# Feed-forward weights quantised in units beside the attention batches, kept in DRAM and loaded in the last one

## What is computed

```python
def fp4_quant_dequant(x):
    xb = x.reshape(shape[:-1] + (shape[-1] // BLOCK, BLOCK))
    scale = jnp.max(jnp.abs(xb), axis=-1, keepdims=True) / 6.0
    scale = jnp.maximum(scale, jnp.float32(1e-12))
    xn = xb / scale
    idx = jnp.searchsorted(_MID, jnp.abs(xn))
    q = _GRID[idx] * jnp.sign(xn) * scale
...
gate = fp4_linear(x, w_gate)
y = fp4_linear(x, w_up)
h = jax.nn.silu(gate) * y
return fp4_linear(h, w_down)
```

## Time and profile before

| | |
|---|---|
| Median of 3 runs | 4076.98 us (4074.86 to 4081.36) |
| The profiled execution | 4073.83 us |
| Its span | 4072.0 us |
| Mean granted TensorE clock | 0.966 |
| PE busy | 3790.2 us (93%) |
| DVE busy | 2592.0 us (64%) |
| ACT busy | 1211.1 us (30%) |
| POOL busy | 930.6 us (23%) |
| Moved by DMA | 302.38 MB, mean 74 GB/s |

### The profile page before, as it was taken

The page is one execution under the profiler, slowest core; times in us unless marked ns, Lnnn a source line. Parts: engine busy times, 40 slices in busy tenths (PEclk is TensorE's granted clock), DMA queues, the critical chain, the costliest instruction groups (busy, mean ns, idle before and its releaser), DMA issues. The chain is left out here.

```text
span 4072.0 us, 63435 instructions
## 1 busy us (share of the span) xinstructions
PE 3790.2 (93%) x21836; PEld 2715.4 (67%) x21836; DVE 2592.0 (64%) x3683; ACT 1211.1 (30%) x2295; POOL 930.6 (23%) x464
## 2 busy tenths in 40 slices
PE   7999999999999999999999727999999999999998
PEld 5556556556565565565565316888888888888887
DVE  4664654655645646646556496777777777777776
ACT  2441432532523514414325222222222222222221
POOL 0451550642533614605516300000000000000000
PEclk9999999999999999999999858999999999999999
DMA  4424424325335244244243220000111010011110
GB/s 150 114 65 148 99 75 146 76 93 141 73 107 132 58 139 116 67 151 94 74 146 76 71 70 16 31 31 31 34 33 33 31 31 31 31 31 31 36 32 28
DMA packets 161754, 302.38 MB, mean 74 GB/s; under 512 B 41072, under 2 KB 43120, under 8 KB 161520
## 3 DMA queue, kind: packets, MB, share of 16 engines
q1 hardware_dynamic: 143088, 265.79, 23.4%
q10 hardware_dynamic: 18432, 33.56, 2.5%
HBM read 196.61 MB, written 101.13 MB: 73 GB/s over the span
## 5 line engine op out<-in xcount | busy, mean ns | idle before, releaser
L1275 PE MATMUL f_ps<-wgu,xqt 128*128 128x512 f32 (+1 forms) x4608 | 994.5, 373 | 17.4 <-DVE h L1130 14.5
L1275 PEld LDWEIGHTS f_ps<-wgu,xqt 128*128 128x128 f32 x4608 | 842.6, 188 | 154.3 <-DVE h L1130 29.9
L668 ACT ACTIVATE pt<-ps_st 128x512 f32<-128x512 f32 (+3 forms) x1152 | 551.7, 527 | 659.8 <-PE ps_st L777 511.9
L502 DVE TENSOR_REDUCE mx<-ps_s 128x1 f32<-128x640 f32 (+3 forms) x576 | 553.4, 961 | 237.9 <-PE ps_s L757 234.7
L439 POOL TENSOR_TENSOR stage<-stage,pt 128x1536 f32<-128x1536 f32 (+2 forms) x176 | 518.2, 2944 | 15.5 <-POOL stage L439 0.5
L1285 PE MATMUL f_ps_o<-wd,hqt 128*128 128x512 f32 x2112 | 512.1, 395 | 2.2 <-DVE hqt L1137 2.2
L437 POOL TENSOR_TENSOR stage<-pt 128x1792 f32<-128x1792 f32 x64 | 258.5, 4040 | 1034.5 <-ACT pt L668 1034.5
L1285 PEld LDWEIGHTS f_ps_o<-wd,hqt 128*128 128x128 f32 x2112 | 392.3, 189 | 80.8 <-DVE hqt L1137 2.6
L728 PE MATMUL ps_dense<-arena,wa 128*128 128x512 f32 x1536 | 401.5, 407 | 8.9 <-DVE rob L550 7.5
L502 DVE TENSOR_REDUCE mx<-ps_dense 128x1 f32<-128x512 f32 x448 | 219.0, 489 | 216.9 <-PE ps_dense L757 211.8
L728 PEld LDWEIGHTS ps_dense<-arena,wa 128*128 128x128 f32 x1536 | 284.7, 192 | 74.1 <-issue 11.7
(11 more groups left out here) (121 smaller groups left out, 4786.9 us busy)
## 6 DMA issues: line engine op xcount, KB each, us to landing
qk_scratch<-stage SPq DMA_DIRECT2D x128, 512.0 KB, 3.0
stack<-qk_scratch SPq DMA_DIRECT2D x192, 256.0 KB
arena<-qk_scratch SPq DMA_DIRECT2D x192, 256.0 KB
xs<-in_L_attn_x SPq DMA_DIRECT2D x64, 256.0 KB, 3.2
rob<-in_L_attn_x ACTq DMA_DIRECT2D x64, 256.0 KB, 2.8
acc_scratch<-rob ACTq DMA_DIRECT2D x64, 256.0 KB, 2.2
xt<-in_L_attn_x SPq DMA_DIRECT2D x64, 256.0 KB, 2.6
at<-acc_scratch SPq DMA_DIRECT2D x64, 256.0 KB, 2.6
```

Of the source, the lines that this page charges most:

```text
L502: nc.vector.tensor_reduce(mx[:, h * ST + q:h * ST + q + 1], scores_bank(p, n)[:, 0:(q + 1) * P], axis=AX.X, op=ALU.max, negate=True).then_ ...
L668: nc.scalar.activation(exps(kt)[:, h, q - kt * P:q - kt * P + n], ps_st[:, w % ST_RING, 0:n], ACT.Exp, scale=SCALE).then_inc(st_exp, 1)
L1275: last = nc.tensor.matmul(ps[:, [0, 1, 1][c], gu, 0:n], xqt[:, a, k], wgu[:, b, gu, k, f:f + n], start=i == 0, stop=i == len(terms) - 1)
```

## The change

The weight stage between the parts is gone, and both parts are one block: `attention` and `feed_forward` now return a function for each engine, and `layer` calls them one after the other inside one block. SBUF tensors are placed by hand (`Memory`), so that tensors of the second part lie over those of the first that are done.

- *Raw copy.* At the start ACT issues six DRAM to DRAM copies of w_gate, w_up and w_down into `raw_scratch`, which holds 33 units of 128 x 512 (8.65 MB in all). SP waits for all six (`q_raw`) at the head of each batch.
- *Units.* Each batch quantises four units, the last one five, with working space in `pt`, which is free outside the head pairs. Two (three in the last batch) stand beside the Q/K/V products: scaled and rounded by DVE in two pieces (`scale_unit`, `round_unit`), ACT's magnitude between them, four PE transposes into `ps_y` (`transpose_unit`), halves by ACT and DVE (`high_of_unit`, `low_of_unit`). Two stand beside the projection. SP stores those beside the products, ACT those beside the projection, each as two halves of 256 KB in `wq_scratch`. SP loads a unit from `raw_scratch`.
- *Loads in the last batch.* ACT issues the loads of `wgu` (11.5 MB) in three pieces: before the head pairs, before pair 6 and before pair 7, and nine of eleven units of `wd` after the last denominators, ahead of the third `res` load. SP loads the last two units of `wd` behind the projection. The first tile of x is quantised beside pair 7.
- *Layout.* `wgu` is now unit by unit; a gate/up product reads four (or three) pieces of 128 columns, 2 KB apart.

The core of the diff, white space apart:

```diff
@@ sync @@
+            sp.wait_ge(q_raw, 6 * DMA)
+            sp.wait_ge(q_lo, ONE + b * PER_BATCH)
+            for i in range(2):
+                load_unit(i)
...
             for i, (g, r, c) in enumerate(QK):
...
+                if i == 6:
+                    store_unit(0)
+                    if final:
+                        load_unit(2)
+                if i == 7:
+                    store_unit(1)
+                if i == 9 and final:
+                    store_unit(2)
...
+            sp.wait_ge(den_full, ONE + b * PAIRS + PAIRS)
+            for i in beside_projection(final):
+                load_unit(i)
@@ vector @@
+            def scale_unit(i):
...
+                link(n, 1, nc.vector.tensor_reduce(sc[:, 0], in_blocks(w), axis=AX.X, op=ALU.max, apply_absolute_value=True))
+                link(n, 2, nc.vector.tensor_scalar(sc[:, 1], sc[:, 0], 1.0 / 6.0, MIN_SCALE, ALU.mult, ALU.max))
+                link(n, 3, nc.vector.reciprocal(sc[:, 2], sc[:, 1]))
+                link(n, 4, nc.vector.tensor_scalar(sc[:, 2], sc[:, 2], TIE, None, ALU.mult))
+                nc.vector.tensor_tensor(in_blocks(t), in_blocks(w), wide(sc[:, 2]), ALU.mult).then_inc(q_t, 1)
...
+                if use == ("V", 2):
+                    scale_unit(0)
+                if use == ("QK", 4):
+                    round_unit(0)
+                if use == ("QK", 5):
+                    scale_unit(1)
+                if use == ("V", 3):
+                    round_unit(1)
+                if use == ("QK", 6):
+                    low_of_unit(0)
+                if use == ("QK", 7):
+                    low_of_unit(1)
+                if final:
+                    if use == ("V", 4):
+                        scale_unit(2)
+                    if use == ("V", 5):
+                        round_unit(2)
+                    if use == ("QK", 9):
+                        low_of_unit(2)
...
             for k in range(ST):
                 add(k)
+                if k == 0:
+                    scale_unit(one)
+                if k == 1:
+                    round_unit(one)
+                if k == 2:
+                    scale_unit(two)
+                if k == 3:
+                    round_unit(two)
+                if k == 4:
+                    low_of_unit(one)
+                if k == 6:
+                    low_of_unit(two)
@@ scalar @@
+        act.dma_start(raw[0:FC].rearrange("u p n -> (u p) n"), w_gate).then_inc(q_raw, DMA)
+        act.dma_start(raw[FC:2 * FC].rearrange("u p n -> (u p) n"), w_up).then_inc(q_raw, DMA)
+        for r in range(KC):
+            act.dma_start(raw[2 * FC:UNITS, :, r * P:(r + 1) * P],
+                          w_down[r * P:(r + 1) * P].rearrange("p (u n) -> u p n", n=P)).then_inc(q_raw, DMA)
...
+            if final:
+                act.wait_ge(v_done, ONE + b * ST + ST)
+                act.wait_ge(qk_lo, ONE + b * NQK + NQK)
+                shared.load_gate_up(act, 0)
             for p in range(PAIRS):
+                if final and p == PAIRS - 2:
+                    shared.load_gate_up(act, 1)
+                if final and p == PAIRS - 1:
+                    shared.load_gate_up(act, 2)
@@ tensor @@
+                if use == ("V", 3):
+                    transpose_unit(0)
+                if use == ("V", 4):
+                    transpose_unit(1)
+                if use == ("QK", 8) and final:
+                    transpose_unit(2)
...
+                if k == 3:
+                    transpose_unit(one)
+                if k == 5:
+                    transpose_unit(two)
@@ feed_forward @@
+    PIECES = [[(0, 0, 2 * FC), (1, 0, 2)], [(1, 2, 16)], [(1, 18, 4)]]
-                        last = nc.tensor.matmul(ps[:, [0, 1, 1][c], gu, 0:n], xqt[:, a, k], wgu[:, b, gu, k, f:f + n],
+                    last = nc.tensor.matmul(ps[:, [0, 1, 1][c], gu, 0:n].rearrange("p (j n) -> p j n", n=P), xqt[:, a, k],
+                                            wgu[:, b, gu * FC + f // P:gu * FC + (f + n) // P, k * P:(k + 1) * P],
```

More of the change, by code:

```diff
@@ new lines, in attention, with w_stage, stack, bank @@
+    DMA = 16
+    LOADS = 7
+    LOADS_AFTER = {6: 5, 7: 2, **{i: 1 for i in range(9, NQK)}}
+    def w_stage(k):
+        return pt[:, (k % 2) * 3 * D:(k % 2 + 1) * 3 * D]
+    def stack(p):
+        s = p % SLOTS
+        return stack01[:, s] if s < 2 else arena[:, s - 2]
+    def bank(kind, i):
+        return ps_dense[:, DN[kind, i] % 2]
+    ob, res = rob[:, 0:2], rob[:, 2:4]
+    dn = ob[:, 0]
+    tail = rob[:, 1:4].rearrange("p a n -> p (a n)")
+    def v_head(t, p, h):
+        first = (2 * p + h) * HD
+        return v[:, t, first:first + HD]
@@ new lines, in body @@
+                    if u == Y_UNIT and p and p < PAIRS - 1:
+                        divide(p - 1)
+            divide(PAIRS - 2)
+            invert_last()
+            divide(PAIRS - 1)
+            if not final:
+                for t in range(XR):
+                    low_of_x(b + 1, t)
+            else:
+                shared.low_of_first(dve)
+            one, two = beside_projection(final)
+            for k in range(ST):
+                add(k)
+                if k == 0:
[10 more added lines that the diff above has]
+                    low_of_unit(two)
@@ L829, in body @@
[L829 to L849 removed]
+                            if kt < summed(p):
+                                src, cols = by_tile(sums(h))[:, s::2], slice(0, QC)
+                            else:
+                                src, cols = exps_of_parity(kt, h, s), y_cols(kt, s)
@@ new lines, in body @@
+                    transposed_scores(p, u, parts - 1)
+                    for n in tiles[ahead:]:
+                        scores(*n)
+                    mask_transposed(p, u, parts - 1)
+                    for n in tiles[ahead:]:
+                        mask_scores(*n)
+            for kt in range(RINGED, ST):
+                times_v(PAIRS - 1, kt)
+            denominators(PAIRS - 1)
+            if not final:
+                for t in range(XR - 1):
+                    transpose_x(b + 1, t)
+            else:
+                shared.transpose_first(pe)
@@ new lines, in feed_forward, with load_gate_up @@
+    x_d, h_d = sem("f_x_d"), sem("f_h_d")
+    PIECES = [[(0, 0, 2 * FC), (1, 0, 2)], [(1, 2, 16)], [(1, 18, 4)]]
+    GATE_UP_LOADS = sum(len(piece) for piece in PIECES)
+    DOWN_LOADS = 6
+    assert 2 * FC == 22 and FC == 11
+    def load_gate_up(act, n):
+        for half, first, units in PIECES[n]:
+            act.dma_start(wgu[:, half, first:first + units].bitcast(F32),
+                          wq[half, :, first:first + units]).then_inc(shared.wgu_in, DMA)
+    shared.load_gate_up = load_gate_up
```

2053 lines of the change are left out of this document (1050 added, 1003 removed).

## The result

The changed kernel takes 4010.22 us (median of 4 runs, 4001.83 to 4014.22) beside 4076.57 for the kernel before on the same chip (4074.86 to 4081.36): a ratio of 0.9833, 95% interval 0.9815 to 0.9850, 66 us or 1.7% less. The forecast was 4023, its range 3978 to 4062. The profiled execution took 4001.83 us (span 4000.0), the shortest of the four.

What follows compares the result with a forecast made beforehand. Before: PE bounds attention and feed-forward, DVE the 156.6 us weight stage between. Terms -159.0 + 49 + 37 + 19 = -54 took the span from 4072.0 to 4018, forecast 4023 us, range 3978 to 4062.

Steps and rivals of the forecast that it cites:

- The gap: Weight quantisation between last projection product and first gate/up product, DVE-bound: all of it goes, -156.6 us.
- The cold clock: First 48 gate/up products: PE no longer starts cold, 11.04 us instead of 13.43, -2.4 us.
- Units beside the batches: Quantising units beside Q/K/V and projection: 3.6 + 1.3 + 1.2 = 6.1 us a batch, +49 over eight; bounds 19 and 72.
- 0.52 MB at 233 GB/s is 2.25 us: Two 256 KB stores ahead of QK7's store delay the first stack's loads 2.25 us, part of a 3.6 us later wait.
- The rooms on DVE: DVE has time for units: 22 us of PE against 16 of DVE in Q/K/V, 2.74 idle of each 3.43 in projection.
- DVE becomes the bound: Rival: units' 5.75 us of DVE and ACT lie on PE's path; all exposed, +87 us, 4164; chance 0.05.
- The copy: Start of batch 0: SP's wait for the 8.65 MB raw copy stops PE from 48.83 to 84.2, +37 us; bounds 18 and 50.
- What would show it: Signs: PE idle about 49 to 84 until QK2's low half; stack wait 5 to 6 us; batches 6 us longer.
- loads block ACT: Rival: in the last batch a large load's issue holds ACT or SP, +20 to 40 us, 4040 to 4062; chance 0.12.
- The last batch: Extra there: third unit 7.5 and 0.6, down loads 5, gate/up loads 6, together +19 us; bounds 4 and 40.
- side costs are small: Rival: copy near 415 GB/s and stack wait hardly later, 3965 to 4000 us; chance 0.22.
- gate/up's operand layout: Rival: wgu's strided pieces slow gate/up by 13 ns a product, 60 us over 4608 products; chance 0.04.

Runs made afterwards that it cites:

- s4_stores_later: Changed kernel with the stores of units 0 and 1 in batches 0 to 6 issued behind QK10's store: 3992.45 us, 0.9780 of the kernel before.
- s1_flat_down: Changed kernel with w_down's four rearranging copies made one flat copy of the same 2.9 MB: 4006.41 us, 0.9815 of the kernel before.
- s1 to s4: Four single edits of the changed kernel: s1_flat_down, s2_no_copy, s4_stores_later, and s3, with SP's copy wait and first unit loads behind QK3's store (4001.53 us).
- l1_third_unit_early: Changed kernel with the final batch's third unit loaded behind QK5's store instead of QK6's: 4001.72 us, 0.9815 of the kernel before.
- s2_no_copy: Changed kernel without raw weight copies or waits for them, units loaded from rows of x instead: 3979.66 us, 0.9748 of the kernel before.
- c1_copy_in_parts: Changed kernel copying only gate and up at the start, one down unit per batch, final down units loaded directly: 3994.82 us, 0.9801 of the kernel before.
- c3_direct_units: Changed kernel with three units per batch straight from the weights, a seven-unit copy, and stores, loads and first-x quantisation re-placed: 3943.20 us, 0.9665 of the kernel before.

## Why the prediction was right, and where it was not

**The gap, -156.6 us:** it is gone whole. **The cold clock, -2.4:** from the first gate/up product to the one that started at 2516.49 before, the same work takes 47.00 us instead of 48.69, so 1.7 came; over the whole feed-forward 0.2 is left.

**Units beside the batches, 6.1 us each, 49 in all:** too high; batches 1 to 6 grew by 3.9. The first score, forecast 3.6 us later in its batch, came 2.7 later. The step that failed is the term "0.52 MB at 233 GB/s is 2.25 us": with the stores moved away (s4_stores_later) the first score comes 1.2 us sooner. That the first stack load goes out 1.3 later was right (1.4 us, though in part by the new wait for QK0's half). The 1.3 us for the clock behind it were 0.5: first score to projection takes 209.2 us instead of 208.7. The 1.2 beside the projection were 0.7. A set of four transposes shows as 0.60 us, but in the projection the product behind it starts 0.44 us after it. The rooms on DVE (22 us against 16; 2.74 of each 3.43) held: no wait of PE that a unit's own pieces on DVE explain shows in batches 0 to 6, and the rival "DVE becomes the bound" fell.

**The copy, +37, plus a batch's 6.1:** batch 0 grew by 29.8, of which 3.9 are a batch's, so 26. The mechanism was in part another one. PE did not stand from 49 to 84 and go on with QK2's half, as "What would show it" has it: it stood from 42.3 to 65.9 until QK0's half was there, then 3.75 us for QK2's, 27.4 in all where 35.4 was forecast. V0 started at 78.00 where 84.2 was forecast. Two errors. The copy was over sooner: SP's wait ends at 70.2, 35 us after the first issue, 247 GB/s for 8.65 MB with the landing in it, where 76.5 was forecast. (By the 207 to 214 GB/s of the Trainium skill, DMA: Bandwidth & Descriptors, Latency and other measured facts, it would have been 41 us; the whole copy went faster.) The forecast took 218 GB/s for all of it. The queues moved 407 from 36 to 44 and 319 from 44 to 54, with the flat copies, and 194 from 55 to 69.8, when w_down's short rows alone were left. And "ACT issues six copies behind its fourth tile" counted the issues as free: they held ACT for 29 us. That this cost only some 5 us beside SP's wait (s1_flat_down) is luck of the forecast, and the 1.6 us for the clock in this term had no row. The text had "loads block ACT" as a rival, but for the last batch, where it did not happen (gate/up's loads were issued in 0.33 to 0.46 us each); the place where it did was not looked at.

**The last batch, +19 and a batch's 6.1:** 30.5 against 25.1 in the profiled execution, 32 to 39 in the runs s1 to s4, which left it alone. The third unit's load: 7.5 forecast; Q/K/V to first score 55.1 where the other batches take 48.9 on average, 6.2, and it is the load (l1_third_unit_early). Gate/up's loads, 6 forecast: a wait of 7.4 to 9.0, and the clock after it; the middle part grew by 12.0 in the profiled execution. Down's loads, 5 forecast: 9.5 over the 28.0 of before, with a second cause that the text did not have: the first x tile's quantisation, moved ahead of the inversion of pair 6's denominators (2273.37 before, 4.3 us behind their copy; now 12.5 us behind it), and behind it the spreading loads, then the down weights. DVE in the changed kernel:

```profile
2343.86 0.69 DVE L598 COPY rob<-ps_dense 128x512 f32<-128x512 f32 x1 [3.22 <-PE ps_dense L1030]
...
2345.89 3.88 DVE L1231 TENSOR_SCALAR xsc<-xsc 128x32 f32<-128x32 f32 x1
...
2356.33 0.24 DVE L602 RECIPROCAL inv<-den 128x16 f32<-128x16 f32 x1
2366.17 1.41 DVE L618 TENSOR_TENSOR yt<-ps_dense,rob 64x512 f32<-64x512 f32 x2 [9.59 <-DMA rob<-inv_scratch]
```

So the sum, -54 for -72, was carried by a right first term. Of the others the batches were 15.7 us too high (seven at 6.1 against 27.0), the copy 11, the last batch 5.4 too low, and the clock and the later start of Q/K/V, 2.2 and 1.3, too low as well: 18 us. Some 27 us too much and 9 too little partly made up for each other. The rival "side costs are small" was not the case (the copy cost 26), nor did gate/up's operand layout matter: 48 later products take 11.05 us, 11.04 before.

## What to carry to other kernels

The work that was moved here cost its new place little (some 1.2 of a batch's 3.9 us are its transposes); what cost were its transfers and where they were issued. Look, for each big transfer that a change adds, at every small one that is issued after it and waited for (here a store of a stage, four rows of denominators, a residual tile), and place it where none follows. And count a DMA's issue as time of the engine that issues it: here it was mostly 0.3 to 0.6 us, but 27.57 for four, and all that stood behind on that engine waited.

When holds lie side by side, taking one away shows little. Take all away once, as s2_no_copy did, before you name any of them as small.

## What the runs showed of the hardware

- **An issue can block.** The two flat copies took ACT 0.70 and 0.59 us, the four rearranging ones 1.4 to 20.1 us each, 27.57 in sum; the same 2.9 MB as a flat copy was issued in 0.61 (s1_flat_down). The profile shows it as the length of the issuing row on ACTq, and "issue" as releaser. That a full queue is what holds the issue is a guess; no run varied it.
- **A short DVE instruction can last as long as POOL's.** L1231 (128x32) takes 0.18 us elsewhere and 3.88 above; it ends at 2349.77, when this row of POOL's ends (2349.74):

```profile
2345.72 4.02 POOL L517 TENSOR_TENSOR stage<-pt 128x1792 f32<-128x1792 f32 x1 [4.02 <-ACT pt L869]
```

  The Trainium skill, SBUF — State Buffer, section Terms, says that the port pair DVE and GpSimd share is "Lock-allocated, exclusive, held for the full instruction"; the two ends agree with that.
- **What follows a wait can cost as much as the wait.** PE waits for pair 2's stack at the same place in nine of the kernels, 7.4 to 9.0 us. In the 38 us behind it the granted clock, as a share of 2.4 GHz, was 0.88 to 0.91 in five of them and 0.74 to 0.75 in four, and the length of the wait doesn't tell which: 8.80 us was followed by 0.88 (c1_copy_in_parts), 8.30 by 0.74 (s4_stores_later). First score to projection took 217.6 to 221.1 in the five and 223.8 or more in the four. It may be why the changed kernel's profiled execution is 8 us under its median; the other executions have no profile.
- **Left open:** what sets that clock; how the 2 us per batch that stay when the stores are moved divide up; and the 6 us that the final batch's middle part in c3_direct_units takes over the other batches' 208.6. Of these, PE's busy time for the same products is 203.6 us against 199.7 in batch 6, at a granted clock of 0.94 against 0.97, and the rest is idle time.
